# Split products for three of the four groups of an attention kernel's output projection

## The reference

```
xn  = layernorm(x)
q, k, v = split(xn @ W_attn + b_attn)
att = softmax(causal(q @ k.T / sqrt(32)))          # per head
out = x + (att @ v) @ W_proj + b_proj
        + fp4_linear(silu(fp4_linear(xn, w_gate)) * fp4_linear(xn, w_up), w_down)
```

## Time and profile before

| | |
|---|---|
| median of three runs | 3647.8 us (3647.26 to 3649.82) |
| profiled execution, its own time | 3647.5 us |
| its span in the trace | 3645.7 us |
| first part (attention) | to 2075 us |
| one batch of it | 254.3 to 255.2 us for the seven before the last, 266.4 us for the last |

### The profile page before, as it was taken

One profiled execution on the slowest core, in us unless ns is written; L12 is line 12 of the kernel. 1 busy time (PEld: TensorE's weight loads), 2 busy tenths in 40 slices (PEclk: granted clock), 3 DMA queues, 4 the chain that ended last, 5 costly groups with the idle time before them and its releaser, 6 DMA issues.

```text
span 3645.7 us, 55788 instructions
## 1 busy us (share of the span) xinstructions
PE 3597.6 (99%) x20748; PEld 2604.6 (71%) x20748; DVE 2610.7 (72%) x3834; ACT 1193.0 (33%) x2249; POOL 1078.4 (30%) x542
## 2 busy tenths in 40 slices
PE   8999999999999999999999999999999999999999
PEld 6557557566566575575565588888888888888887
DVE  6776766766767767767667577777777777777776
ACT  2542533533524515425325322222222222222222
POOL 0760952833825717608518300000000000000000
PEclk9999999999999999999999999999999999999999
DMA  6525436336255255254355500111011101110110
GB/s 195 133 77 183 110 115 177 83 119 181 64 168 150 66 186 129 80 183 101 120 167 156 202 26 29 35 35 32 29 35 35 32 29 35 35 32 29 35 35 29
DMA packets 180445, 336.13 MB, mean 92 GB/s; under 512 B 42688, under 2 KB 50368, under 8 KB 179392
## 3 DMA queue, kind: packets, MB, share of 16 engines
q1 hardware_dynamic: 156096, 280.47, 27.1%
q10 hardware_dynamic: 24192, 53.49, 4.3%
HBM read 213.92 MB, written 118.43 MB: 91 GB/s over the span
## 4 chain that ended last, share of the span: by engine, by line
PE 90%; issue 3%; POOL 2%; DVE 2%; DMA 1%; ACT 1%; SPq 0%; POOLq 0%; ACTq 0%; DVEq 0%
PE f_ps L1570 26%; PE ps_dense L1056 13%; PE f_ps_o L1582 13%; PE ps_st L1113 8%; PE ps_s L1081 5%; PE ps_dense L1227 5%; PE ps_y L1139 4%; PE ps_dense L1139 3%; PE ps_dense L1081 2%; PE ps_dense L1151 2%; PE f_ps L1562 1%; POOL stage L615 1%; PE ps_st L1122 1%; PE ps_s L1086 1%; POOL stage L613 1%
## 5 line engine op out<-in xcount | busy, mean ns | idle before, releaser
L1570 PE MATMUL f_ps<-wgu,xqt 128*128 128x512 f32 (+1 forms) x4608 | 992.7, 373 | 1.4 <-DVE xqt L1430 1.4
L1570 PEld LDWEIGHTS f_ps<-wgu,xqt 128*128 128x128 f32 x4608 | 842.5, 188 | 122.7 <-DVE xqt L1430 1.7
L967 ACT ACTIVATE pt<-ps_st 128x512 f32<-128x512 f32 (+3 forms) x1152 | 540.8, 525 | 489.9 <-PE ps_st L1113 335.3
L683 DVE TENSOR_REDUCE mx<-ps_s 128x1 f32<-128x640 f32 (+3 forms) x512 | 524.1, 1024 | 164.2 <-PE ps_s L1086 163.6
L1582 PE MATMUL f_ps_o<-wd,hqt 128*128 128x512 f32 x2112 | 513.4, 396 | 0.2 <-DVE hqt L1456 0.2
L1582 PEld LDWEIGHTS f_ps_o<-wd,hqt 128*128 128x128 f32 x2112 | 392.6, 189 | 79.5 <-DVE hqt L1456 0.6
L1056 PE MATMUL ps_dense<-arena,wa 128*128 128x512 f32 x1536 | 384.3, 400 | 0.0
L615 POOL TENSOR_TENSOR stage<-stage,pt 128x1536 f32<-128x1536 f32 (+2 forms) x128 | 378.9, 2960 | 16.6 <-ACT pt L967 6.3
L613 POOL TENSOR_TENSOR stage<-pt 128x1792 f32<-128x1792 f32 x48 | 192.7, 4014 | 615.9 <-ACT pt L967 563.9
L1056 PEld LDWEIGHTS ps_dense<-arena,wa 128*128 128x128 f32 x1536 | 281.9, 189 | 58.0 <-issue 3.8
L683 DVE TENSOR_REDUCE mx<-ps_dense 128x1 f32<-128x128 f32 (+3 forms) x424 | 204.4, 482 | 90.5 <-PE ps_dense L1086 90.5
(11 more groups left out here) (145 smaller groups left out, 5295.1 us busy)
## 6 DMA issues: line engine op xcount, KB each, us to landing
qk_scratch<-stage SPq DMA_DIRECT2D x128, 512.0 KB, 2.8
stack<-qk_scratch SPq DMA_DIRECT2D x192, 256.0 KB
arena<-qk_scratch SPq DMA_DIRECT2D x192, 256.0 KB
xs<-in_L_attn_x SPq DMA_DIRECT2D x64, 256.0 KB, 3.9
rob<-in_L_attn_x ACTq DMA_DIRECT2D x64, 256.0 KB, 2.9
acc_scratch<-rob ACTq DMA_DIRECT2D x64, 256.0 KB, 2.1
xt<-in_L_attn_x SPq DMA_DIRECT2D x64, 256.0 KB, 2.6
at<-acc_scratch SPq DMA_DIRECT2D x64, 256.0 KB, 2.7
```

The costliest lines, as they stand in the source:

```text
L683: nc.vector.tensor_reduce(mx[:, h * ST + q:h * ST + q + 1], scores_bank(p, n)[:, 0:(q + 1) * P], axis=AX.X, op=ALU.max, negate=True).then_ ...
L967: nc.scalar.activation(exps(kt)[:, heads[0], q - kt * P:q - kt * P + n], ps_st[:, w % ST_RING, 0:n], ACT.Exp, scale=SCALE).then_inc(st_exp, 1)
L1570: last = nc.tensor.matmul(ps[:, SLOT[c], gu, 0:n].rearrange("p (j n) -> p j n", n=P), xqt[:, a, k], wgu[:, b, gu * FC + f // P:gu * FC + ( ...
```

## The change

For all batches but the last, groups 0 to 2 of the projection become split products: `yt_high` (float32r) is made by ScalarE in 128x512 copies (`high_of_y`, four in pair 6 after key tiles 0 to 3, two after pair 7's exponentials), the low part by GpSimd in 128x1024 differences in place (`low_of_y`, groups 0 and 1 after pair 6's sums, group 2 after pair 7's). Group 3 stays in float32. W_proj's halves are made once, in the first batch, stored to `wp_scratch` by ScalarE's queue and loaded by SyncE in pair 6 of each batch (two DMAs of 768 KB) into stack slot 0, which is no longer used by then; `yt_high` lies in slot 1.

The projection has three banks (`OUT_BANKS`), the third in `ps_s`, and all three have their first groups made ahead of pair 7's division. There are six residual buffers (`RES`), four of them in `stage`, all loaded after pair 7's denominators.

In these batches the sums of pair 6 lie in the fourth row of stack slots 0 and 1 (`left01`), and wait for no denominators; those of pair 7 lie in `stage` and wait for pair 5's denominators. GpSimd sums five key tiles for pair 7, as for pair 6. The last batch keeps two residual buffers, the float32 projection and three key tiles for pair 7. GpSimd's batches are written out in line and not as a loop.

```diff
-    ST_RING, SLOTS, XR = 3, 4, 4
+    ST_RING, SLOTS, XR, RES = 3, 4, 4, 6
-    def summed(p):
-
-        return ST if p < PAIRS - 2 else RINGED if p < PAIRS - 1 else 3
+    def summed(p, final):
+
+        return ST if p < PAIRS - 2 else 3 if p == PAIRS - 1 and final else RINGED
...
+    left01 = memory.over("left01", [P, 2, 4, S], F32, "stack01")
+    yt_low = memory.over("yt_low", [P, G, S], F32R, "yt")
...
+    SPLIT = G - 1
+
+    def wp_halves(slot):
+        return stack01[:, slot].rearrange("p a (c n) -> p (a c) n", n=D)[:, 0:2 * SPLIT]
+
+    yt_high = stack01[:, 1, 0:SPLIT]
...
+    OUT_BANKS = 3
+
     def bank(kind, i):
+        if kind == "P":
+            return [ps_dense[:, 0], ps_dense[:, 1], ps_s[:, QC:S]][i % OUT_BANKS]
         return ps_dense[:, DN[kind, i] % 2]
...
+    def sums_place(p, final):
+        return 1 if p in X_SUMS else 2 if p == PAIRS - 2 and not final else 0
+
+    def summed_in(p, final):
+
+        return max((k for k in range(p) if sums_place(k, final) == sums_place(p, final)), default=None)
...
+                if i == GROUP0:
+
+                    sp.wait_ge(p_out, 2 * DMA)
...
+                if p == PAIRS - 2 and not final:
+                    sp.wait_ge(st_exp, ONE + b * PAIRS * NPARTS + (PAIRS - SLOTS + 1) * NPARTS)
+                    for half in range(2):
+                        sp.dma_start(wp_halves(0)[:, half * SPLIT:(half + 1) * SPLIT].bitcast(F32),
+                                     wp_scratch[half]).then_inc(p_in, DMA)
...
+            if b == 0:
+                pool.wait_ge(p_hi, 1)
+                nc.gpsimd.tensor_tensor(wp_halves(1)[:, SPLIT:], wp[:, 0:SPLIT], wp_halves(1)[:, 0:SPLIT].bitcast(F32),
+                                        ALU.subtract).then_inc(p_lo, 1)
+
+            def low_of_y(g):
+                pool.wait_ge(y_hi, ONE + b * SPLIT * 2 + (g + 1) * 2)
+                nc.gpsimd.tensor_tensor(yt_low[:, g], yt[:, g], yt_high[:, g].bitcast(F32), ALU.subtract).then_inc(y_lo, 1)
...
-                if SUMMED_IN[p] is not None:
-                    pool.wait_ge(den_full, ONE + b * PAIRS + SUMMED_IN[p] + 1)
-                for kt in SUM_ORDER[:summed(p) - 1]:
+                if summed_in(p, final) is not None:
+                    pool.wait_ge(den_full, ONE + b * PAIRS + summed_in(p, final) + 1)
+                for kt in SUM_ORDER[:summed(p, final) - 1]:
                     sum_up(p, kt)
+                if p == PAIRS - 2 and not final:
+                    for g in range(SPLIT - 1):
+                        low_of_y(g)
+                if p == PAIRS - 1 and not final:
+                    low_of_y(SPLIT - 1)
...
+            def high_of_y(n):
+
+                g, cols = n // 2, slice(n % 2 * QC, (n % 2 + 1) * QC)
+                act.wait_ge(y_div, ONE + b * PAIRS * 2 + (g + 1) * 4)
+                nc.scalar.activation(yt_high[:, g, cols], yt[:, g, cols], ACT.Copy).then_inc(y_hi, 1)
...
+                    if p == PAIRS - 2 and kt < (SPLIT - 1) * 2 and not final:
+                        high_of_y(kt)
...
+            else:
+                for n in range((SPLIT - 1) * 2, SPLIT * 2):
+                    high_of_y(n)
             act.wait_ge(den_full, ONE + b * PAIRS + PAIRS)
-            for k in range(2):
+            for k in range(2 if final else RES):
                 load(k)
...
+                if kind == "P" and i >= OUT_BANKS:
+                    pe.wait_ge(o_sum, ONE + b * ST + i - OUT_BANKS + 1)
+                    return
...
+                    terms = [(yt[:, g, rows], wp[:, g])]
+                    if not final and g < SPLIT:
+                        high, low = yt_high[:, g, rows], yt_low[:, g, rows]
+                        terms = [(high, wp_halves(0)[:, g]), (high, wp_halves(0)[:, SPLIT + g]), (low, wp_halves(0)[:, g])]
...
-            for k in range(2):
-                pe.wait_ge(y_div, ONE + b * PAIRS * 2 + (PAIRS - 2 + k) * 2)
+            if not final:
+                pe.wait_ge(p_in, ONE + (b + 1) * 2 * DMA)
+                pe.wait_ge(y_lo, ONE + (b + 1) * SPLIT)
+            for k in range(OUT_BANKS):
+                pe.wait_ge(y_div, ONE + b * PAIRS * 2 + (PAIRS - 2 + min(k, 1)) * 2)
                 emptied("P", k)
                 output(k, range(G - 1))
```

More of the change, by code:

```diff
@@ L82, in attention @@
     TAIL = 2 * P * sum(ST - k for k in range(RINGED, ST))
-    def summed(p):
-        return ST if p < PAIRS - 2 else RINGED if p < PAIRS - 1 else 3
+    def summed(p, final):
+        return ST if p < PAIRS - 2 else 3 if p == PAIRS - 1 and final else RINGED
     SUM_ORDER = [*range(1, ST)]
     FREED = {0: 1, 1: 1, 2: 2, 3: 3, 4: 4}
-    SUMS0 = [sum(summed(k) - 1 for k in range(p)) for p in range(PAIRS)]
-    SUMS = SUMS0[-1] + summed(PAIRS - 1) - 1
+    SUMS0 = [sum(summed(k, False) - 1 for k in range(p)) for p in range(PAIRS)]
+    SUMS = SUMS0[-1] + summed(PAIRS - 1, False) - 1
     TILES = 2 * ST
@@ L240, in attention @@
     y_div = sem("a_y_div")
-    res_in = [sem(f"a_res_in{i}") for i in range(2)]
+    y_hi, y_lo = sem("a_y_hi"), sem("a_y_lo")
+    p_hi, p_lo, p_out, p_in = sem("a_p_hi"), sem("a_p_lo"), sem("a_p_out"), sem("a_p_in")
+    res_in = [sem(f"a_res_in{i}") for i in range(RES)]
     o_res = sem("a_o_res")
@@ L283, in attention, with sums, both_sums @@
     X_SUMS = (1, 3)
[L284 to L292, removed]
+    def sums_place(p, final):
+        return 1 if p in X_SUMS else 2 if p == PAIRS - 2 and not final else 0
+    def summed_in(p, final):
+        return max((k for k in range(p) if sums_place(k, final) == sums_place(p, final)), default=None)
+    def sums(p, h, final):
+        return both_sums(p, final)[:, h]
+    def both_sums(p, final):
+        return [stage[:, :, :, :].rearrange("p h a n -> p h (a n)"),
+                xs[:, :, :].rearrange("p (h a) n -> p h (a n)", h=2),
+                left01[:, :, 3]][sums_place(p, final)]
     def by_tile(a):
@@ L628, in body @@
                 x_and_bias(t)
-        batches(pool, body)
+        batches_in_line(body)
     def vector(dve):
@@ L917, in body @@
                     high_of_unit(1)
+                if (kind, i) == ("QK", 5) and b == 0:
+                    act.wait_ge(p_lo, 1)
+                    for half in range(2):
+                        act.dma_start(wp_scratch[half],
+                                      wp_halves(1)[:, half * SPLIT:(half + 1) * SPLIT].bitcast(F32)).then_inc(p_out, DMA)
                 if (kind, i) == ("QK", 8) and final:
@@ L1150, in denominators @@
                     for h in range(2):
-                        last = nc.tensor.matmul(by_tile(den_bank(p)[y_rows(h, s)]), ones[:, :], by_tile(sums(p, h))[:, s::2],
-                                                start=True, stop=summed(p) == ST)
-                for kt in range(summed(p), ST):
+                        last = nc.tensor.matmul(by_tile(den_bank(p)[y_rows(h, s)]), ones[:, :], by_tile(sums(p, h, final))[:, s::2],
+                                                start=True, stop=summed(p, final) == ST)
+                for kt in range(summed(p, final), ST):
                     for s in range(2):
@@ L1224, in output @@
             def output(k, groups):
-                t = OUT[k]
+                rows = slice(OUT[k] * P, (OUT[k] + 1) * P)
                 for g in groups:
-                    last = nc.tensor.matmul(bank("P", k), yt[:, g, t * P:(t + 1) * P], wp[:, g, :],
-                                            start=g == 0, stop=g == G - 1)
+                    terms = [(yt[:, g, rows], wp[:, g])]
+                    if not final and g < SPLIT:
+                        high, low = yt_high[:, g, rows], yt_low[:, g, rows]
+                        terms = [(high, wp_halves(0)[:, g]), (high, wp_halves(0)[:, SPLIT + g]), (low, wp_halves(0)[:, g])]
+                    for i, (left, right) in enumerate(terms):
+                        last = nc.tensor.matmul(bank("P", k), left, right, start=g == 0 and i == 0,
+                                                stop=g == G - 1 and i == len(terms) - 1)
                 if g == G - 1:
```

55 lines of the change are left out of this document (36 added, 19 removed).

## The result

The kernel with the change took 3699.6 us (median of 4 runs, 3696.5 to 3702.9) beside 3648.8 us for the kernel before (4 runs, 3647.3 to 3650.0): ratio 1.014, 95% interval 1.0124 to 1.0156. It is 51 us slower; the forecast was 36 us slower, and the measured time lies at the upper edge of its range (3658 to 3700). The profiled execution took 3702.1 us, its span is 3700.3.

What follows compares the result with a forecast made beforehand. TensorE, busy for 99% of the span, was taken as the bound. Per batch +4.3 (late GpSimd sums, shorter denominators) - 1.6 (projection) + 2.4 (clock) = +5.1; seven batches 35.7 plus 0.5 one-off: 3684 us, range 3658 to 3700.

Steps and rivals of the forecast that it cites:

- GpSimd's order: End of batch: pair 7's four sums run from 240.0 to 253.1, so TensorE stands still about 5.3 us.
- The start of the denominators: Pair 7's denominators on TensorE start 5.8 us later per batch, because GpSimd's sums are late.
- Denominators and first fall of the clock: Pair 7's denominators take 1.5 us less; half clock after the wait for GpSimd costs 2.4 us a batch, bounds 0 to 3.0.
- After R: From VectorE's reciprocal of pair 7's denominators (R) to next batch: 28.5 us for 30.1, with 2.8 us wait at unit's transposes.
- rival 4: Clock falls a second time in the 2.8 us wait at the unit's transposes: 2.4 us more a batch, 3701; chance 0.09.
- The sum: Per batch +4.3 - 1.6 + 2.4 = +5.1 us; seven batches 35.7, one-off 0.5: +36, 3684 us.
- The last batch: The last batch keeps its float32 projection and was forecast to change by 0.
- Buffers and banks: Projection: six residual buffers worth nothing, as TensorE has no gap there; three banks give VectorE slack on adds.
- The rival in which GpSimd is in time: Pair 7's sums are done when TensorE comes: 3.1 us a batch, 22 us faster, 3626; chance 0.09.
- the 30 us: Projection: split products save 0.53 us a tile, 4.2 us a batch, 30 us in all, if TensorE can use it.

Runs made afterwards that it cites:

- first experiment: Kernel after the change, with GpSimd summing three key tiles for pair 7 again in every batch: 3658.9 us, ratio 1.0036 to the kernel before.
- the filled wait: Kernel after the change, with 20 products of constants on TensorE ahead of pair 7's denominators: 3686.0 us, ratio 1.0112 to the kernel before.
- The filled second wait: Kernel after with three key tiles for pair 7, plus 13 products of constants ahead of the first unit's transposes: 3652.7 us, ratio 1.0013.
- the best version: Kernel after with three key tiles for pair 7 and only TensorE's unit transposes one tile later: 3630.8 us, ratio 0.9951 to the kernel before.

## Why the prediction was right in sign and 15 us short

**GpSimd's order: right.** The first sum of pair 7 was put at 240.0 and the end of the fourth at 253.1; they were at 241.33 and 254.48. The 1.4 us are the start: pair 6's first sum began at 221.89 and not at 220.8, behind a first batch in which TensorE waits 1.23 us for a norm before any of this. The differences took 4.71 us (4.8 forecast), the last three sums 8.98. The wait was 4.45 us in the fifth batch and 4.71 to 4.73 in the other six, against 5.3; TensorE too came later than forecast, at 249.82 for 247.9. That it is the larger part of the loss was shown from both sides: without it 41 us less, with it alone 32 us more.

**The start of the denominators: 0.8 us a batch too small.** The forecast moved it by 5.8, the runs by 6.6. A wait in front of them also ends an overlap: with three tiles the first products with the sums start at 248.26, ahead of y's last six at 248.36 (first experiment), so the move is the wait and some 0.6 us of that overlap. Of what is left, 0.2 a batch is the start-up; some 0.8 us between the QK products and the denominators is there with three key tiles too (221.7 us against 220.9 in the batches behind the first). Some 0.5 of it is a wait that the prediction doesn't have and the kernel before didn't have: TensorE stands ahead of the denominators of pair 0, in each of the seven batches, for GpSimd's last sum.

```profile
128.00 1.07 PE L1233 MATMUL ps_dense<-stage,ones 128*32 128x512 f32 x8 [0.52 <-POOL stage L667]
```

GpSimd's seven sums of pair 0 took 17.50 us from the first's start to the last's end (110.44 to 127.94), where they took 17.11 before (109.71 to 126.82, and TensorE came at 126.87): the pauses between them are longer. What made them so was not tested; the batches of GpSimd being written out in line is one candidate.

**Denominators and first fall of the clock: right.** The clock fell in all seven waits. The fall costs 2.2 us on the mean by the filled wait (1.5 to 2.8), forecast 2.4, bounds 0 and 3.0. The trace of the kernel before held a nearer row than those of the earlier trace rows, which the prediction passed over:

```profile
1859.13 1.01 PE L1081 MATMUL ps_s<-stack 96*128 96x512 f32 x2 [5.59 <-DVE mx L683]
```

In that idle time of the last batch the clock fell at 1855.7, 2.2 us after TensorE stopped, and was back at 1862.5.

The 1.5 us that five tiles save on the denominators were there at full clock (2.05 us to R).

**After R: the mechanism right, its clock not.** VectorE's chain bound TensorE at the unit's transposes, forecast 2.8 us of wait, measured 2.5 to 3.4. In the two batches with one fall of the clock the stretch from there to the next batch took 12.65 us, against 12.5 worked out. In the other five it took 13.7 to 13.8: the clock fell a second time. **This is the step that failed:** rival 4, with a chance of 0.09, happened in 5 batches of 7, though at 1.15 us each and not 2.4. I had held the 2.8 us wait beside rows of which one fell after 2.79 us (and 1.41 more), one within 2.39 us, and one did not after 2.73, and should have given the second fall even odds. The filled second wait shows its price by itself, 6 us. That 3699.6 stands next to rival 4's 3701 is luck in part: the second fall gives only 6 of the 15 us that are missing.

**The sum.** Per batch +7.1 for +5.1 makes 14 of the 18 us by which the profiled execution missed (54.6 for 36.2): 5 to 6 of them ahead of the denominators, 2 between them and the unit's transposes, and 6 in the second fall. The last batch, forecast at 0, took 8.5 more and the feed-forward 2.7 less. The 8.5 us belong in the main to this one execution: the kernel with the filled first wait has the same last batch, and from its first QK product to the transposes of L1652 behind it that took 285.5 us, 0.5 more than before, where the kernel after took 293.5; with three key tiles it took 286.4 and without norms 289.8. In the kernel after, TensorE waited 1.90 us at 2033.87 on a chain that began with a late transfer of denominators, and ran at half clock behind it.

**Buffers and banks: "worth nothing" held only while another wait stood in front.** The prediction priced the six residual buffers at 0 because TensorE had no gap there. In the version without the other waits they are worth 14 us. The rival in which GpSimd is in time was put at 3626; the best version has GpSimd in time, VectorE's chain out of the way, and 3630.8.

**Where the 30 us went.** The projection's products are cheaper by 4.2 us a batch, 29 us in all. 41 us go to the key tiles that GpSimd took over, 28 to the unit's transposes standing one tile too early for the faster tiles in front of them (22 wait, 6 clock), and that is more than there was to gain. With both undone 18 of the 29 us arrive. In the profiled executions R to the next batch is 3.6 us shorter instead of 4.2 (4 us lost in all), and 1.3 a batch goes back ahead of the denominators (9 us, of which 1.5 is only that the first QK product started 1.5 us sooner, at 25.24). The last batch, whose transposes this edit moves too though its tiles are float32, takes 3.1 us more than before up to the transposes of L1648 behind it, but from its first QK product to the end of the program both kernels take 1837 us.

## What to carry to other kernels

When work moves to an engine with a low busy share, add up its list from the last thing it had to wait for up to the next thing that another engine asks of it; two sums on a 30% busy GpSimd cost 32 us here. When a stage gets faster, work out again where each of its consumers' and suppliers' chains meets it: the transposes had 1 us to spare, the faster tiles ate it, and moving them by one tile was worth 28 us. Price a wait of TensorE with its clock, and do not price a buffer at nothing while another wait hides it.

## What the runs showed of the hardware

Taking away one fall of the clock did not take away the other. With both waits open the clock fell in or just behind the second wait in 5 batches of 7; with TensorE kept busy through the first wait it fell there in 6, and with three key tiles, which leave no first wait, in 5. In the kernel before with five key tiles it fell in or just behind 7 of 8 waits of 3.41 us. Waits of 2.5 to 3.4 us were followed by half clock in most cases and not in all, in the same place of the same program, so a forecast for such a wait is a chance and not a yes or no. The Trainium skill (TensorE: Matmul & The Clock Gate, section HAM oscillation) says that pauses between bursts bring the throttle back; the seven falls in the 4.7 us waits agree, and the shorter ones agree in part.

VectorE's four norms (L702, one tensor input each) took 10.95 us, where they took 3.07 in the kernel before. GpSimd's sums beside them, in narrower stretches of the same timeline:

```profile
249.10 2.89 POOL L667 TENSOR_TENSOR stage<-stage,pt 128x1280 f32<-128x1280 f32 x1
...
252.13 2.34 POOL L667 TENSOR_TENSOR stage<-stage,pt 128x1024 f32<-128x1024 f32 x1
```

and VectorE's norms there:

```profile
249.16 3.11 DVE L702 TENSOR_SCALAR xs<-xs,mv 128x512 f32<-128x512 f32 x1
...
252.19 2.56 DVE L702 TENSOR_SCALAR xs<-xs,mv 128x512 f32<-128x512 f32 x1
```

One norm ends about 0.15 us after the next sum has started, at 249.24 for 249.10, and the next norm starts with it: each lasts as long as a sum of GpSimd. In the kernel before the first norm took 1.70 us, until GpSimd's only sum there was done, and the other three followed at steps of 0.46. GpSimd's sums are not slowed: three took 8.98 us beside the norms and 8.98 in the run without them. The difference behind them took 2.53 us beside the last norm and 2.35 without it. The Trainium skill (GPSIMD Engine Reference, section Specifications) has GpSimd share its SBUF interfaces with VectorE, with contention for VectorE instructions that have two SBUF inputs or run in a mode that uses two ports. These rows show contention for an instruction with one input, and that it goes by whole instructions; whether that one ran in a mode with two ports no row shows. That it cost the kernel's time nothing was shown by taking the norms out.
